# An earlier split of the queries in the large attentions, and the low halves of the key weights made by GpSimd

## What is computed

```python
qh = (q_in @ wq + bq).reshape(b, q_len, H, K)          # H = 16, K = 128
kh = (kv_in @ wk + bk).reshape(b, t, H, K)
vh = (kv_in @ wv + bv).reshape(b, t, H, K)
kh = jnp.concatenate([kh, jnp.broadcast_to(bias_k, (b, 1, H, K))], axis=1)
vh = jnp.concatenate([vh, jnp.broadcast_to(bias_v, (b, 1, H, K))], axis=1)
logits = jnp.einsum('bqhk,bthk->bhqt', qh, kh) / scale
weights = jax.nn.softmax(logits, axis=-1)
ctx = jnp.einsum('bhqt,bthk->bqhk', weights, vh).reshape(b, q_len, H * K)
return ctx @ wo + bo
```

## Time and profile before

| | |
|---|---|
| median of 3 runs | 2334.54 us (2333.76 to 2337.82) |
| the profiled execution | 2336.15 us, its span 2334.0 us |
| mean granted TensorE clock | 0.993 |
| busy, share of the span | PE 96%, DVE 59%, ACT 48%, POOL 26% |
| chain that ended last | PE 77%, DVE 8%, DMA 6%, SP's queue 3%, issue 3%, ACT 2% |
| DMA | 480.05 MB, 206 GB/s over the span |

### The profile page before, as it was taken

How to read it: one execution, slowest core, us unless ns; L and a number is a source line. 1 busy time by engine, 2 the same in 40 slices (tenths; PEclk the granted TensorE clock), 3 DMA queues, 4 the chain that set the end, 5 groups by cost and what they waited for, 6 DMA issues and landing times.

```text
span 2334.0 us, 36291 instructions
## 1 busy us (share of the span) xinstructions
PE 2240.0 (96%) x12347; PEld 2013.1 (86%) x12347; DVE 1369.5 (59%) x3102; ACT 1115.3 (48%) x2282; POOL 602.6 (26%) x913
## 2 busy tenths in 40 slices
PE   7999999999999899999999999999999999999999
PEld 6777788898999899889888898999889899888888
DVE  6877773515666566556554516666565565555743
ACT  5777743434444454445453434445445445453421
POOL 2111065321212322312312301223123123113421
PEclk9999999999999999999999999999999999999999
DMA  5322246566877978977964547887987888864210
GB/s 196 134 89 102 65 133 204 184 203 208 285 235 255 294 232 262 298 231 249 294 198 152 202 163 243 275 265 245 275 267 246 272 270 251 264 192 148 59 55 32
DMA packets 325464, 480.05 MB, mean 206 GB/s; under 512 B 65567, under 2 KB 249779, under 8 KB 323235
## 3 DMA queue, kind: packets, MB, share of 16 engines
q1 hardware_dynamic: 325282, 477.73, 64.2%
HBM read 368.72 MB, written 108.92 MB: 205 GB/s over the span
## 4 chain that ended last, share of the span: by engine, by line
PE 77%; DVE 8%; DMA 6%; SPq 3%; issue 3%; ACT 2%; ACTq 0%; DVEq 0%
PE ps_o L1869 7%; PE ps_o L1871 7%; PE ps_o L1870 7%; PE ps_k L1869 5%; PE ps_k L1870 5%; PE ps_k L1871 5%; PE ps_v L1869 5%; PE ps_v L1871 5%; PE ps_v L1870 5%; PE ps_t L1870 4%; PE ps_s L1869 4%; PE ps_t L1871 4%; PE ps_t L1869 4%; PE ps_s L1871 3%; PE ps_s L1870 3%
## 5 line engine op out<-in xcount | busy, mean ns | idle before, releaser
L1246 ACT ACTIVATE prob<-ps_s,row_columns 128x376 f32<-128x376 f32 x256 | 146.4, 572 | 339.4 <-DVE row_columns L1641 339.4
L934 POOL CAST k_hi<-xk_hi 128x1 fp32r<-128x1 f32 x256 | 48.3, 189 | 913.0 <-PE ps_s L1871 913.0
L941 POOL TENSOR_TENSOR pt_lo<-pt_lo,pt_hi 128x512 fp32r<-128x512 f32 x186 | 243.9, 1338 | 135.2 <-ACT pt_hi L1211 135.2
L1869 PE MATMUL ps_k<-cs_hi,w_a_hi 128*128 128x376 f32 x636 | 222.5, 350 | 0.0
L1870 PE MATMUL ps_k<-cs_lo,w_a_hi 128*128 128x376 f32 x636 | 217.9, 343 | 0.0
L1871 PE MATMUL ps_k<-cs_hi,w_a_lo 128*128 128x376 f32 x636 | 216.5, 340 | 0.0
L1526 DVE RECIPROCAL row_columns<-row_columns 128x1 f32<-128x1 f32 (+1 forms) x384 | 62.5, 163 | 248.4 <-ACT prob L1246 240.8
L889 POOL TENSOR_TENSOR w_b_lo<-w_raw_b,w_b_hi 128x512 fp32r<-128x512 f32 x80 | 108.1, 1378 | 358.3 <-ACT w_b_hi L991 358.1
L1659 DVE STREAM_TRANSPOSE blocks<-prob 128x384 f32<-128x384 f32 x248 | 143.5, 578 | 96.4 <-DMA turned_probabilities<-blocks 89.2
L1529 DVE TENSOR_SCALAR prob<-prob,row_columns 128x375 f32<-128x375 f32 (+1 forms) x384 | 179.1, 466 | 4.5
L1870 PE MATMUL ps_t<-cs_lo,w_a_hi 128*128 128x376 f32 x512 | 170.7, 333 | 0.0
(11 more groups left out here) (290 smaller groups left out, 6298.8 us busy)
## 6 DMA issues: line engine op xcount, KB each, us to landing
ckd<-context_by_key_halves SPq DMA_DIRECT2D x256, 384.0 KB, 5.3
cs_hi<-context_halves SPq DMA_DIRECT2D x64, 752.0 KB, 6.0
cs_lo<-context_halves SPq DMA_DIRECT2D x64, 752.0 KB, 7.6
turned_probabilities<-blocks SPq DMA_DIRECT2D x62, 768.0 KB, 4.5
pt_lo<-turned_probabilities SPq DMA_DIRECT2D x248, 192.0 KB, 3.8
w_raw_b<-in_blocks_b SPq DMA_DIRECT2D x104, 256.0 KB, 3.9
w_raw_a<-in_blocks_a SPq DMA_DIRECT2D x104, 256.0 KB, 5.3
q<-q_scratch SPq DMA_DIRECT2D x64, 256.0 KB, 4.1
```

What stands on the lines that cost most here:

```text
L934: pool.tensor_copy(k[t % 2][0][:, LK:KW], xk[0][:, ds(col, 1)])
L941: pool.tensor_tensor(lo, lo.bitcast(F32), hi, ALU.subtract).then_inc(t_lo, 1)
L1246: act.activation(prob[buf][:, 0:KW], ps_s[buf][:, 0:KW], ACT.Exp, bias=max_neg[:, buf:buf + 1], accum_out=prob_sum[:, buf:buf + 1]).then_i ...
L1869: pe.matmul(out, w_h, m_h, start=first, stop=False)
```

## The change

```diff
@@ Attention.__init__
         self.split_slots = {(NB - 1, t): t for t in range(NT)} if layer == 0 else {
-            (NB - 2, 2): 0, (NB - 2, 3): 1, (NB - 1, 0): 2, (NB - 1, 1): 3}
+            (NB - 2, 2): 0, (NB - 2, 3): 1, (NB - 1, 1): 2, (NB - 1, 2): 3}
@@ GpSimd, attend, one_batch
                         if t == 1 and place.before():
                             turned_lo(place.before())
+                        if place.split_column(t) is not None:
+                            split_lo(0, place.block_a + 1, [place.split_column(t)])
                         split_lo(1, place.block_b, place.split_own(t))
@@ ScalarE, attend, one_batch
-                        if t == 0 and place.before():
-                            turned_hi(place.before())
+                        if t == 0 and not place.final:
+                            split_q(place.next())
                         if place.final and t < 2:
                             last_turned_hi(place, t)
                         if place.key(t + 2):
                             exp(*place.key(t + 2))
+                        if t == 0 and place.before():
+                            turned_hi(place.before())
                         if place.split_column(t) is not None:
...
-                        if t == 1 and not place.final:
-                            split_q(place.next())
@@ VectorE, attend, one_batch (the last batch of an attention keeps its order)
-                        for summed, d in chunks(place, t):
+                        for summed, d in () if place.final else chunks(place, t)[:-1]:
                             sum_lo(summed, d)
...
                         if place.key(t + 2):
                             maximum(*place.key(t + 2))
+                        for summed, d in () if place.final else chunks(place, t)[-1:]:
+                            sum_lo(summed, d)
+                        if place.key(t + 2):
                             normalized_1(*place.key(t + 2))
                         if query_piece(place, t):
                             last_query(query, a, skip, query_piece(place, t))
-                        if place.split_column(t) is not None:
-                            split_lo(0, place.block_a + 1, [place.split_column(t)])
-                        if t == 1 and not place.final:
+                        if t == 0 and not place.final:
                             split_q(place.next())
@@ TensorE, attend, scores
                     pe.wait_ge(k_extra, place.tile + t + 1 - ATT1.tile0)
-                    if t == 0:
-                        pe.wait_ge(q_lo, place.batch + 1)
@@ TensorE, attend, prologue: before the first scores
+                            pe.wait_ge(q_lo, place.batch + 1)
@@ TensorE, attend, one_batch, before key(t + 3)
+                        if t == 2 and not place.final:
+                            pe.wait_ge(q_lo, place.batch + 2)
                         if place.key(t + 3):
                             key(*place.key(t + 3))
```

More of the change, by code:

```diff
@@ L1705, in one_batch @@
                             output(quad_before(place), head)
-                        for summed, d in chunks(place, t):
+                        if place.final:
+                            for summed, d in chunks(place, t):
+                                sum_lo(summed, d)
+                                if t == 2 and d < 2:
+                                    last_turned_lo(place, d + 2)
+                            if t < 2:
+                                last_turned_lo(place, t)
+                        for summed, d in () if place.final else chunks(place, t)[:-1]:
                             sum_lo(summed, d)
-                            if place.final and t == 2 and d < 2:
-                                last_turned_lo(place, d + 2)
-                        if place.final and t < 2:
-                            last_turned_lo(place, t)
                         if place.key(t + 2):
                             maximum(*place.key(t + 2))
+                        for summed, d in () if place.final else chunks(place, t)[-1:]:
+                            sum_lo(summed, d)
+                        if place.key(t + 2):
                             normalized_1(*place.key(t + 2))
```

## The result

| | before | after |
|---|---|---|
| median of 4 runs, us | 2334.15 (2332.32 to 2337.82) | 2295.99 (2294.67 to 2299.39) |
| ratio | | 0.9837, 95% interval 0.982 to 0.9854 |
| profiled execution, its span, us | 2336.15, 2334.0 | 2299.39, 2297.5 |
| mean granted clock | 0.993 | 0.990 |

The forecast was 2290.5 with a range of 2279 to 2314: 38.2 us were gained between the medians where 44.2 were summed. The profiled execution is the slowest of the four; between the two profiled executions 36.8 us were gained. The lines of the kernel have moved by two to six: `product`'s matmuls are L1875 to L1877, the q is L1524, the exponential L1248, the transposition L1661.

A forecast was written before the change was run, and what follows sets the result against it. TensorE's work plus its gaps was taken as the bound, the largest wait being scores for the queries' low half. Terms -39.2 - 7.0 - 2.5 + 2.0 + 1.5 + 1.0 = -44.2 gave 2290.5 us, range 2279 to 2314.

The forecast's parts named there:

- Split of the queries, -39.2: TensorE's waits for q: splitting one step earlier removes 48.7 us, less 9.5 not gained, so 39.2 us.
- slack of q, forecast 0.9: Plain batch: q done at 880.07, 0.9 us before TensorE asks for it, where it was 0.3 late.
- What isn't gained, 9.5: Six q waits at batch 3's transfer chain (7.5 us) return as batch 4 k_lo waits; two more of 1.0.
- two more of 1.0: End of each attention's first batch: two further q waits of 1.0 us, counted as not gained.
- The clock, -7.0: Half-clock stretches beside q waits: five of 3.41 us are won at about 1.4 each, 7.0 us in all.
- 1 us: Batch 4: its longer single wait may bring one or two more half-clock stretches, costing 1 us.
- Exponential and maximum, -2.5 and +2.0: ScalarE and VectorE orders: small k_lo and sum waits go, 2.5 us; later pt_hi costs 2 in a few batches.
- Weight columns, +1.5: 32 key weight columns moved to GpSimd: 1.5 us cost in all, bounds 0 and 1.3 in each of six batches.
- A: Transfers take half back: pt_lo late by 0.5 us in 45 batches, 22.5 of the gain lost, 2313; chance 0.19.
- B: GpSimd's pt_lo first: q held 1.3 us, the wait only moves and pt_lo waits are added, 2357; chance 0.06.
- C: No change: transfer chains bind everywhere as in batch 4, every q wait becomes another, 2334.5; chance 0.05.

The follow-up runs named there:

- e2: Kernel before with only the two orders (exponential ahead of pt_hi, maximum ahead of the last sum_lo): 2320.42 us, ratio 0.9894.
- e3: Kernel before with only the 32 weight columns moved from VectorE to GpSimd, with new slots: 2335.35 us, ratio 0.9957.
- e10: Changed kernel with the queries' split back in step 1 and TensorE's wait back in the scores: 2312.00 us, ratio 0.9846.
- e1: Kernel before with only the queries' split moved one step up, with TensorE's wait: 2379.13 us, ratio 1.0143.
- e11: Changed kernel with the 32 weight columns back on VectorE in their old slots: 2331.16 us, ratio 0.9930.
- e7: Changed kernel with pt_hi ahead of the exponential of step 0 again: 2369.68 us, ratio 1.0092.
- e9: Changed kernel with the next group's weights fetched at the end of step 0 of batches 2 and 6, not in batch 3: 2265.10 us, ratio 0.9647.
- e8: Changed kernel with VectorE's maximum behind all sum_lo again: 2304.88 us, ratio 0.9816.

## Why the prediction was right, and where its steps were not

**What bounds the kernel.** Right: TensorE's gaps, and among them the q. Why q was late in a bad batch was read in part (an exponential behind pt_hi and its transfer): with the orders alone 7.9 of the 14.2 us in the batches 7 stay (e2), and without the weight column ahead of q none does (e3). The working then gave the cure to the wrong edit.

**Split of the queries, -39.2.** As a sum for the whole change it came out (both with 0.17 for each broken pipeline): the waits for q with their broken pipelines went from 48.7 to 5.6 + 3 x 0.17 = 6.1, that is 42.6 less, and the slack of q, forecast 0.9, is 1.03. As the price of the split it was wrong. The working put the exponential at 1.39 us behind its scores before it costed the split, so the split got what the order does. The parts, as ratios to the kernel before:

| | columns on VectorE | columns on GpSimd |
|---|---|---|
| split in step 1, orders as before | 1 | 0.9957 (e3) |
| split in step 1, new orders | 0.9894 (e2) | 0.9846 (e10) |
| split in step 0, orders as before | 1.0143 (e1) | not run |
| split in step 0, new orders | 0.9930 (e11) | 0.9837, 0.9828 (the change) |

The orders and the columns add up: 0.9894 x 0.9957 is 0.9851, and e10 has 0.9846. The split, which the prediction gave nearly all of the gain, shows no gain in any row that is clear of the noise: alone it costs 33 us, with the new orders and the columns on VectorE 8 (e2 and e11, whose intervals don't overlap), and in the whole change it is worth 0.1 to 0.2%, within the noise. It needs the order: without it q in step 0 is late by pt_hi's 1.4 us and by what it loses beside GpSimd (e7).

**What isn't gained, 9.5.** Right for the batches 4, if short: k_lo's waits there went from 7.6 to 17.2 us, 9.6 more where 7.5 were forecast, and k_lo in all from 8.9 to 21.1. The "two more of 1.0" at the end of the first batches did go (17.43 to 16.39 us each). In their place the batches 1 of the first groups grew by 2.3 together: in the first attention a transposition waits there 4.27 us for the store of batch 0, and q waits 2.32 in place of 1.15.

**The clock, -7.0.** Wrong in sign for the whole. The stretches of the trace at 0.50, the 1.2 GHz level, add up to 34.3 us before and to 44.4 after (mean clock 0.993 and 0.990). The 13.7 us beside the q waits of the batches 7 are gone, as forecast, but more came elsewhere: 10.2 beside the two 4.36 us waits of the last batches, 3.4 each in one more batch 1, behind a wait of 1.80 for a sum in a batch 5, and ahead of the first attention, where nothing was changed. Those beside the batches 4 are 20.5 where they were 17.1. One of their stretches (us; PE, PEld, DVE, ACT, POOL busy; clock, DMA share, GB/s):

```profile
1956.90:1963.70 6.80, 6.08 (x19) 5.96 (x20) 6.26 (x16) 4.00 (x8) 0.43 (x2) 0.50 0.89 256
```

At the prediction's own price (2.3 us for 6.83) 10.1 us more at half clock are 3.4 lost where 7.0 were to be won: 10.4 us between them, more than the 7.4 by which the sum missed in the profiled execution. That price is 1.15 for a stretch of 3.41, not the 1.4 that the prediction then used, so its five stretches were worth 5.8. The "1 us" for a longer single wait in batch 4 was right: five of the six waits (2.21 to 3.47) stand beside a stretch at half clock, the one of 2.70 does not, and the 3.4 us more are 1.1 at that price. The term lacked the last batches. With the long waits taken away the clock is 0.996 (e9).

**Exponential and maximum, -2.5 and +2.0.** The exponential's order was mis-sized most: it decides between 0.983 and 1.009 (e7). The maximum's is worth nothing that can be told (e8). pt_lo did not grow in the plain batches, as forecast: from 11.9 to 9.9, but 8.7 of that are the two last batches, which no term covered and which are 5.8 us longer.

**Weight columns, +1.5.** Wrong in sign: 10 us gained alone (e3), 22 with the rest (e11). The prediction saw that VectorE loses eight of them from ahead of a q and booked that under the first term without a price. It had read 1.16 for such an instruction beside GpSimd; it did not see that the wait for the column's high half and a q of 1.75 behind it come on top once q stands in step 0.

**The total.** That the sum came within 7.4 us with its parts so far off is partly luck. Against the clock and the last batches stood terms that came out better than booked: the q waits by 3.4, and the 2.0 for pt_lo and the 1.5 for the columns, which no wait in the trace asks for. And the parts were measured together, so that it didn't matter which edit the 39.2 was booked under.

**The rivals.** A did not come: no pt_lo wait in plain batches. B's mechanism is real, but it decides by order. Its total is matched by luck: it forecast 2357 from a q held for 1.3 us and a late pt_lo, and e7's ratio is 2356 with pt_hi's 1.47, a q only 0.51 longer and next to no wait for pt_lo. In the changed kernel VectorE's q comes first (0.65); in e1 and e7 GpSimd's pt_lo does (1.18 and 1.12 on average over all 64), and both are slower than the kernel before. This is what the Trainium skill, page "SBUF — State Buffer", section "Who interferes with whom", states: the engine that issues first keeps the shared ports for its whole instruction and the other waits. The runs agree, with q as the second at 1.15 us and as the first at 0.65, and with its end 0.55 behind the end of the subtraction that was running (e7). B was given 6%; the kernel stands 0.14 us from it. C is excluded: the interval of the ratio ends at 0.9854.

## What to carry to other kernels

When a change moves one step earlier and reorders its neighbours, cost each edit with the others absent: the one that carries the gain may be one that looks like tidying, here an exponential that no longer stands behind a copy that waits for a transfer, and a weight column that no longer stands ahead of the queries. When a wait is named for the last thing to arrive, ask how much of the rest would surface if it went; here a burst of eight transfers ahead of an urgent store was worth as much as the whole change, and moving it needed one changed condition. And look at the special last iteration by itself: it had an order of its own, and the edit that suited the other 62 batches made the two last ones wait.

## What the runs showed of the hardware

The scaling of the probabilities on VectorE, which reads one tensor in SBUF, is held beside GpSimd as well. Its 256 instructions took 549 ns on average in the changed kernel and 470 before; in e7 467:

```profile
L1531 DVE TENSOR_SCALAR prob<-prob,row_columns 128x375 f32<-128x375 f32 x256 | 140.7, 549 | 0.0
```

In the changed kernel 82 of them overlapped a subtraction of GpSimd's; these took 0.85 us on average and 1.47 at most, the others 0.41. The order that protects q in step 0 puts the scaling of step 1 beside pt_lo; no wait of TensorE's names it. And the time to issue a transfer depends on where it stands: the same four took SyncE 4.49 us in batch 3 and 2.58 in batch 2, each time with the transfers' engines busy (a DMA share of 1.02 in the 4.49 us, and of 1.03 in the 6.4 us from 902.39). What sets this was not tried.
